# Layer 2 cross attention: queries and keys read in place, the loop written out, a bank of its own for values and a later output step

## The reference, cut to what matters

```
def _L2_xattn_ref(x, mem_seq, mem_mask, rms_scale, q_w, kv_w, out_w):
    xn = _rmsnorm(x, rms_scale)
    mn = _rmsnorm(mem_seq, rms_scale)
    q = jnp.einsum('BTD,NDH->BTNH', xn, q_w)
    kv = jnp.einsum('BSD,cKDH->cBSKH', mn, kv_w)
    k, v = (kv[0], kv[1])
    ...
    q = _apply_rope(q, q_pos) * HEAD_DIM ** (-0.5)
    k = _apply_rope(k, k_pos)
    logits = jnp.einsum('BTKGH,BSKH->BKGTS', q, k, preferred_element_type=jnp.float32)
    masked = jnp.where(mem_mask[:, None, None, None, :], logits, MASK_FILL)
    probs = jax.nn.softmax(masked, axis=-1).astype(x.dtype)
    enc = jnp.einsum('BKGTS,BSKH->BTKGH', probs, v).reshape(B, T, NUM_HEADS, HEAD_DIM)
    return jnp.einsum('BTNH,NHD->BTD', enc, out_w)
```

## Time and profile before

| what | us |
|---|---|
| runs of the kernel, median of 3 (lowest to highest) | 2555.1 (2549.35 to 2555.91) |
| the profiled execution, its own time | 2565.78 |
| its span, from first to last instruction | 2564.0 |
| this attention stage in it, from 1424.9 to 1513.2 | 88.3 |

### The profile page before, as it was taken

How to read it: one execution, slowest core, us unless ns; L and a number is a source line. 1 busy time by engine, 2 the same in 40 slices (tenths; PEclk the granted TensorE clock), 3 DMA queues, 4 the chain that set the end, 5 groups by cost and what they waited for, 6 DMA issues and landing times. The chain is left out here.

```text
span 2564.0 us, 36910 instructions
## 1 busy us (share of the span) xinstructions
PE 1901.9 (74%) x11783; PEld 1134.4 (44%) x11795; DVE 1735.5 (68%) x5543; ACT 1147.0 (45%) x3159; POOL 712.8 (28%) x620
## 2 busy tenths in 40 slices
PE   6997899854877999979987886556565655555777
PEld 2654446442445666654454554333332333332443
DVE  4325342267765656647745557999999999995655
ACT  3652532251315666641142564555545454544421
POOL 1200045014432333320033320444333333332130
PEclk8988899965988999989988898676656665666978
DMA  5000101400000000000010000000000000000000
GB/s 208 2 1 1 43 10 29 152 9 1 2 2 1 2 1 0 1 1 0 22 71 1 1 1 1 1 1 1 1 1 1 1 1 1 1 1 1 1 1 17
DMA packets 10591, 37.76 MB, mean 15 GB/s; under 512 B 1344, under 2 KB 7488, under 8 KB 9136
## 3 DMA queue, kind: packets, MB, share of 16 engines
q1 hardware_dynamic: 8880, 33.04, 3.4%
q0 software_dynamic: 1536, 2.59, 0.4%
HBM read 30.15 MB, written 5.51 MB: 14 GB/s over the span
## 5 line engine op out<-in xcount | busy, mean ns | idle before, releaser
L3674 PE MATMUL psum<-work 32*128 32x256 f32 x512 | 131.7, 660 | 294.0 <-ACT work L3784 294.0
L3843 DVE MATCH_REPLACE8 work<-work 128x256 f32<-128x256 f32 x768 | 325.7, 516 | 0.0
L3891 POOL TENSOR_TENSOR work<-work 128x1024 f32<-128x1024 f32 x64 | 150.7, 2354 | 494.2 <-ACT work L3784 488.1
L3840 DVE MAX8 work<-work 128x8 f32<-128x256 f32 x768 | 286.4, 512 | 0.0
L3674 PEld LDWEIGHTS psum<-work 32*128 32x128 f32 x512 | 78.5, 314 | 320.6 <-ACT work L3784 163.2
L693 POOL TENSOR_TENSOR work<-work 128x256 f32<-128x256 f32 (+2 forms) x144 | 133.5, 946 | 266.1 <-DVE work L953 266.1
L883 ACT ACTIVATE work<-work 128x128 f32<-128x128 f32 (+1 forms) x320 | 145.6, 456 | 40.9 <-PE psum L753 25.0
L3843 DVE MATCH_VALUE_LOAD work<-work 128x8 f32 x768 | 142.4, 185 | 0.0
L3784 ACT ACTIVATE work<-work 128x256 f32<-128x256 f32 x256 | 129.0, 504 | 0.0
L3697 PE MATMUL psum<-work,tiles 128*8 128x256 f32 x512 | 116.1, 606 | 13.6 <-ACT work L3793 13.6
L3893 POOL TENSOR_TENSOR work<-work 128x1024 f32<-128x1024 f32 x64 | 121.2, 1894 | 6.1 <-DVE work L3865 1.2
(11 more groups left out here) (619 smaller groups left out, 4708.3 us busy)
## 6 DMA issues: line engine op xcount, KB each, us to landing
big_weights<-L0f_dram SPq DMA_DIRECT2D x1, 6117.5 KB, 28.8
big_weights<-L_dram SPq DMA_DIRECT2D x1, 5772.0 KB, 17.7
big_weights<-L_dram SPq DMA_DIRECT2D x1, 4952.5 KB, 16.4
choice_rows<-tiles SPq DMA_DIRECT2D x2, 1024.0 KB, 10.4
tiles<-choice_rows SPq DMA_DIRECT2D x8, 256.0 KB, 5.1
big_weights<-L_dram SPq DMA_DIRECT2D x1, 2027.0 KB, 21.9
big_weights<-L_dram SPq DMA_DIRECT2D x1, 1630.5 KB, 13.5
big_weights<-L0f_dram SPq DMA_DIRECT2D x1, 1630.5 KB, 6.4
```

Source lines behind the costliest of these rows:

```text
L3674: mm = nc.tensor.matmul(scores(n)[:, u, :], qb[head, tile % 2, u % 2 * P:(u % 2 + 1) * P], kb[head, tile % 2, :], start=True, stop=True, t ...
L3840: ch.step(v.max(top8[:, n % 2, u, r, :], src[:, u, :]))
L3843: ins = v.match_replace(raw[:, n % 2, u, :], top8[:, n % 2, u, r, :], src[:, u, :], REPLACED)
L3891: ch.link(g.tensor_tensor(mine, mine, rest[:, n % 2], ALU.subtract))
```

## The change

With `ready_qk`, which only this stage sets: the scores are computed straight from `c.T`, so K, Q and the two copies L849 are not issued, and every wait on them goes. The loop is replaced by a Python loop that writes the steps out. V is written to the upper half of bank 7 instead of bank 6. `OUT` becomes `MIX` + 2 for the output product and its addition, so that these come one step later, while C stays at `MIX` + 1 (now `COPY`). V now waits for the copy of the last values and for the last output addition. M waits for the copy of its values and, at the first group of a sequence, for C of the sequence before. O waits for C, for the values' copy and for the addition before.

```
-    OUT = MIX + 1
+    COPY = MIX + 1
+    OUT = COPY + 1 if ready_qk else COPY
...
+    value_bank = c.psum[:, 7, S:2 * S] if ready_qk else c.psum[:, 6, :]
...
+    def sequence_rows(x, it, g, base, lo, n):
+        return x[base:base + rows, bass.ds(seq_of(it, g) * S + lo, n)]
...
         steps(0, True, 0, W)
-        with eng.Fori(1, NIT) as it:
-            steps(it, False, 0, W)
+        if ready_qk:
+            for it in range(1, NIT):
+                steps(it, False, 0, W)
+        else:
+            with eng.Fori(1, NIT) as it:
+                steps(it, False, 0, W)
...
-                    if starts_tile(g):
+                    if starts_tile(g) and not ready_qk:
                         pe.wait_ge(c.qk_taken.sem, queries_taken(it, g))
...
+                        if ready_qk:
+                            mm = nc.tensor.matmul(scores(g)[:, u, :], sequence_rows(q_src, it, g, base, half.start, P),
+                                                  sequence_rows(k_src, it, g, base, 0, S), start=True, stop=True,
+                                                  tile_position=(base, 0))
+                            continue
...
-                if g < W and starts_tile(g):
+                if g < W and starts_tile(g) and not ready_qk:
...
-                    pe.wait_ge(c.qk_taken.sem, queries_taken(it, g) - 1)
+                    if not ready_qk:
+                        pe.wait_ge(c.qk_taken.sem, queries_taken(it, g) - 1)
+                    elif ok(g - NG):
+                        pe.wait_ge(c.v_taken.sem, after(c.v_taken, "v", it, val_n(g - NG)))
+                        if ok(g - OUT - 1):
+                            pe.wait_ge(c.out_added.sem, after(c.out_added, "o", it, out_n(g - OUT - 1)))
...
-                        mm = nc.tensor.matmul(bank(6)[:, kt * vw:(kt + 1) * vw],
+                        mm = nc.tensor.matmul(value_bank[:, kt * vw:(kt + 1) * vw],
...
-                    if g < W and starts_values(g):
+                    if ready_qk:
+                        pe.wait_ge(c.v_taken.sem, after(c.v_taken, "v", it, val_n(m)))
+                        if m % vg == 0 and ok(m - 1):
+                            pe.wait_ge(c.out_copied.sem, after(c.out_copied, "o", it, out_n(m - 1)))
+                    elif g < W and starts_values(g):
...
-                        if g < W and starts_tile(g):
+                        if ready_qk:
+                            pe.wait_ge(c.v_taken.sem, after(c.v_taken, "v", it, val_n(min(g, W - 1))))
+                            if ok(o - vg):
+                                pe.wait_ge(c.out_added.sem, after(c.out_added, "o", it, out_n(o) - 1))
+                        elif g < W and starts_tile(g):
...
-                o = t - OUT
+                o = t - COPY
...
-                    src = bank(6)[:, 0:2 * vw].rearrange("p (t h e) -> p t h e", t=2, e=dh)
+                    src = value_bank[:, 0:2 * vw].rearrange("p (t h e) -> p t h e", t=2, e=dh)
...
-                    mask=lambda mb, qt: mb, prepare_mask=prepare, mask_words=S, shared_kv=True, still_values=True)
+                    mask=lambda mb, qt: mb, prepare_mask=prepare, mask_words=S, shared_kv=True, still_values=True, ready_qk=True)
```

More of the change, by code:

```diff
@@ L561, in attention_stage @@
                     head_scale=None, mask=None, prepare_mask=None, mask_words=0, shared_kv=False, top=0,
-                    residual2=None, skip_max=False, still_values=False, causal=False):
+                    residual2=None, skip_max=False, still_values=False, causal=False, ready_qk=False):
     nc = c.nc
@@ L721, in step @@
                         base = (h % per_tile) * pitch
+                        half = slice((u % 2) * P, (u % 2 + 1) * P)
+                        if ready_qk:
[3 more added lines that the diff above has]
+                            continue
                         q = qb[base:base + rows, tile_n(g) % 2, :]
                         k = kb[base:base + rows, tile_n(g) % 2, :]
-                        half = slice((u % 2) * P, (u % 2 + 1) * P)
                         lhs, rhs = (k[:, half], q) if skip_max else (q[:, half], k)
@@ L1001, in attention_stage @@
     groups, outs = B * NG, B * NG // vg
-    for s, n in ((c.staged, B), (c.qk_ready, 2 * groups // gpt), (c.qk_taken, 2 * groups // gpt),
+    tiles_taken = 0 if ready_qk else 2 * groups // gpt
+    for s, n in ((c.staged, B), (c.qk_ready, tiles_taken), (c.qk_taken, tiles_taken),
                  (c.v_ready, B * per["v"] // SQ), (c.v_taken, B * per["v"] // SQ), (c.scores_ready, groups),
```

## The result

The changed kernel takes 2544.06 us (median of 6 runs, 2540.86 to 2548.38), the one before beside it 2555.07 (6 runs): a ratio of 0.9961, 95% interval 0.9946 to 0.9976. That is faster by 11.0 us, or 0.43%, which is only a little more than the 0.3% that can be told from no change. The forecast was 2544.0.

A forecast was written before the change was run, and what follows sets the result against it. PE was taken as nearest the bound, with a loop through K's wait for C on ACT setting 9.51 us a sequence. Terms -2.6 - 1.2 - 7.5 - 1.6 + 1.8 = -11.1 took 2555.1 to 2544.0 us, range 2539.5 to 2552.

The forecast's parts named there:

- One sequence: Middle of the stage: a sequence falls from 9.51 to 8.0 us, set by a chain through DVE and POOL.
- The loop before: Kernel before: 9.51 us a sequence set by K, ACT's copies, T's copy, E and C again.
- PE's wait: New rhythm: PE still waits 0.87 us once a sequence, for POOL's N before T.
- The short chain: Chain of the half with V in place of O, 7.6 us, shorter than the 8.01 of the other.
- The start: Stage start to the fifth group's scores: 2.6 us gained at the first N, then 1.2, 3.8 earlier.
- The middle: Fifth to fifteenth group's scores: 7.5 us gained over five sequences, plus 1.6, half of two stretches at 1.2 GHz.
- The end: Stage end: 1.8 us given back, 1.5 by the last two groups' scores and 0.3 by the last output products.
- The added waits and the loop: Waits of V, M and O covered, at most 2.5 us over six sequences if not; writing the loop out 0.
- Behind the stage: Later stages start at another time against the clock's changes; 2 us added to the range below 2541.4.
- The clock did not stay low: Rival: without K and Q PE may stay at 1.2 GHz; 6 in 100 to slower by over 0.3%.
- The wait did move: Rival: the 1.40 gap returns before M, 8.54 us a sequence, 2548; 17 in 100, together with more low-clock stretches.
- third rival: Copies L849 were hidden anyway and the later output eats the rest: within 2 us of 2555; 5 in 100.

The follow-up runs named there:

- mask in place: Changed kernel without DVE's mask copy L3371, the reductions reading the mask where it lies: 2542.2 us (1 run), ratio 0.997.
- two kernels: Changed kernel with the loop kept: 2540.8 us, ratio 0.9955; kernel before with only this stage's loop written out: 2552.2 us, ratio 1.000.

## Why the prediction was right

- **One sequence.** Forecast 9.51 to 8.0 by the chain S, X, V's copy, R, N, T, M, O; measured 7.94, link by link within 0.06 of the forecast. The experiments show the chain from both sides: N shorter by 0.85 gives 0.75, products of 0.5 a sequence ahead of T cost 0, K and Q ahead of S 0.86.
- **The loop before.** The prediction had 9.51 run through K, ACT's copies, T's copy, E and C. The rows of before say otherwise for two of these. The E ahead of C had waited 0.81 for DVE's row maxima and not for a copy:

```profile
1470.16 0.51 ACT L883 ACTIVATE work<-work 128x256 f32<-128x256 f32 x1 [0.81 <-DVE work L928]
...
1472.15 0.35 ACT L843 COPY work<-psum 128x256 f32<-128x256 f32 x1
```

  The loop runs through S and X: S to X 1.26, X to E 1.90, E 1.99, C to K 0.40, and from K over Q, T, V, M and O to the next S 3.96 (1463.04 to 1467.00), 9.51 in all. K, Q and the wait for C are in it, as the prediction needed. The copies L849 are not, so in the middle of the stage their removal gave nothing; only at the start did V wait for one (2.4 us, once). The forecast did not hang on this step, since it summed the new chain and not the old.
- **PE's wait.** Forecast once a sequence, 0.87; measured twice, 0.31 and 0.28 in the rows. The short chain was forecast at 7.6 and came to 7.93, because the mask copy, 0.28 us alone, takes 1.63 where it now falls beside N and delays X by 0.34. The trace of before already had one such copy, which starts 0.98 into an N:

```profile
1445.07 1.89 POOL L693 TENSOR_TENSOR work<-work 128x1024 f32<-128x1024 f32 x1 [4.13 <-DVE work L953]
...
1446.05 1.05 DVE L3343 COPY work<-tiles 128x256 f32<-128x256 f32 x1
```

  This is a miss in what surrounds the chain that set the time, without effect on it (mask in place: 7.94, with one wait of 0.68).
- **The start.** Forecast -2.6 at the first N; measured 10.26 to 6.85 after the stage's start, -3.4. The first S came 1.7 sooner (forecast 1.5), and from there to N it took 5.84 instead of 7.57, 1.7 less where 1.1 was forecast. These scores took 1.52 instead of 2.11, 0.6 less: they ran, in part, ahead of the fall of the clock (0.96 up to 1417.5), which is luck. From the third to the fifth group's scores it gained 1.0 where 1.2 was forecast. At the fifth group's scores that makes -4.1 against a forecast of -3.8.
- **The middle.** Forecast -7.5 and -1.6, measured 50.81 to 40.96, -9.9. Five sequences gave 5 x 1.57 = 7.9. Both later stretches at 1.2 GHz are gone, of which I had taken half; but the early one reaches to 1438.0, 5 us into this part, and costs 1.3 of the 3.26 there. So the half came out about right (2.0 for 1.6), by luck and in another way.
- **The end.** Forecast +1.8, measured +0.94 (16.07 to 17.01 from the fifteenth group's scores). The term was over-sized: the wait for N is split between both steps, so the last two scores are 4.06 apart and not 4.6, 0.98 more than the 3.08 of before, and the second output's wait of 0.61 for the addition adds nothing to the total that shows.
- **The added waits and the loop**, forecast 0: no row of PE after waits for C, for V's copy or for an addition in the middle of the stage. The loop is 0 by two kernels. (The prediction has both sequences around its start at 9.51. That holds from scores to scores; K's starts there are 11.16 apart, with a stretch at 1.2 GHz between them.) By the rule of the Trainium skill (Runtime: NRT & Kernel Launch, Instruction fetch mechanics) that full unrolling is preferred there would have been something; no run here shows it, for a body that runs once.
- **Behind the stage**, forecast 0 within 2 us: +1.3.
- **The rivals.** The clock did not stay low: 20.5 us of the stage at 1.2 GHz, and 52.9 at 2.4. The wait did move, from C at K to N at T, but is smaller, 0.73 for 1.40; no gap ends with M on C. Of the third rival one half holds, since the copies were hidden in the middle of the stage. What was not hidden are the products and the wait for C, and the later output gives more (1.67 over the five sequences) than it takes (0.95 at the end).
- **Two figures that don't follow.** With both later stretches gone the prediction's own terms give -12.7; the further 1.0 to -13.7, for an early return of the clock, stands on no row. And six sequences that each take 5 us more add 30 to 77.2, which is 107 us and not 103. Neither enters the sum.

The sum was -11.1. The terms as measured are -4.1, -9.9 and +0.94, which make -13.05, and +1.3 behind the stage. The mechanism was right, but that the total was right to 0.1 us is partly luck: the start and the middle were forecast 0.3 and 0.8 too small, the loss at the end 0.9 too large, the 1.3 behind the stage worked against all three, and the medians, with an interval of about 4 us either way, can't tell 11.1 from 11.7.

What stays open is what sets the length of the early stretch at 1.2 GHz: 13.7, 17.1, 20.5, 23.9 and 26.9 us in kernels whose first twenty microseconds are much alike (but for the added products in those of 17.1 and 26.9). It moves the stage by 1 to 3 us, about as much as each of the smaller edits, and no kernel here was made to tell its cause. The 9.2 us ahead of the stage in the profiled execution of before were not pursued either.

## What to carry to other kernels

The engines' busy shares name the candidates for the bound, but they don't say what a change is worth. That is the difference between the longest chain that it cuts and the next one. Sum both from rows, link by link, from one instruction to its own successor in the next round, and check that the links add up to the time of the round. The prediction didn't do that for the loop before and had two links of it wrong. The place of an instruction on a queue decides its price: products cost their whole issue between the chain's last link and its next head, and others, somewhat shorter, cost nothing in the pause where their engine waits for another. Once such a pause is seen, move off-chain work into it; here that took another 0.64 us off a sequence, after the 1.57 of the change, without removing anything but a copy.

## What the runs showed of the hardware

DVE's copy of the mask (128x256, both sides in SBUF) takes 0.28 us alone and 1.63 beside POOL's multiply of 1.89. It ends each time shortly behind POOL's instruction: N ends at 1451.45 (1449.56 + 1.89) and the copy at 1451.60. With N cut to 1.04 (1442.59 to 1443.63) the copy takes 0.77 and ends at 1443.78, again 0.15 behind. DVE's other work beside N was not lengthened: X's reductions, which read PSUM and one tile in SBUF, take 0.42 and the copy out of PSUM 0.66 to 0.69, with N running or not (the reductions whole inside an N in the kernel before). The Trainium skill (SBUF — State Buffer, Who interferes with whom) says that DVE, in a mode with two ports that a copy can enter, and POOL share a pair of ports, and that the instruction issued first holds it for its whole length while the other waits. The trace agrees for a copy behind N, with 0.15 between the two ends. That POOL waits for a copy issued first is not shown: N took its 1.89 at 1422.49 too, 0.11 before the end of a copy that had started ahead of it. A copy between two SBUF tiles on DVE should be costed with POOL's instruction beside it, not by its mean in a profile where it happened to stand alone.

Reading a 32-row slice of a long tile in place of a compact copy cost PE nothing: the eight matmuls of S took 1.14 us from the copies and 1.14 from the tiles, both at full clock.
